# Self-attention of a decoder's second block: four score products of a batch in one group, and the sums of the softmax from TensorE

## The reference, cut to what matters

```
x = x @ Wq + bq (and Wk, Wv); q, k turned by rope
scores = jnp.einsum('bhqd,bhkd->bhqk', q, k) / np.sqrt(D_K)
probs = jax.nn.softmax(scores, axis=-1)
attn = jnp.einsum('bhqk,bhkd->bhqd', probs, v)
x = _layernorm(x + attn @ Wo + bo)
```

## Time and profile before

| | us |
|---|---|
| median of 3 runs | 2189.8 (2188.1 to 2191.36) |
| profiled execution | 2189.22 |
| its span | 2187.4 |
| granted clock of PE, mean | 0.947 |

### The profile page before, as it was taken

One profiled execution on the slowest core, in us unless ns is written; L12 is line 12 of the kernel. 1 busy time (PEld: TensorE's weight loads), 2 busy tenths in 40 slices (PEclk: granted clock), 3 DMA queues, 4 the chain that ended last, 5 costly groups with the idle time before them and its releaser, 6 DMA issues.

```text
span 2187.4 us, 46524 instructions
## 1 busy us (share of the span) xinstructions
PE 1948.0 (89%) x16008; PEld 1493.8 (68%) x16008; DVE 1409.0 (64%) x3579; ACT 1272.1 (58%) x4630; POOL 449.0 (21%) x777
## 2 busy tenths in 40 slices
PE   3549999999999999999689999889997777699998
PEld 1227888888888888888456767656665444467775
DVE  4776777777777777777356566467776577354443
ACT  2215666666666667776334444379997788133333
POOL 2101111111111111111222122034443233011110
PEclk8769999999999999999889999989999899599999
DMA  7000000000000000000200000010000000000000
GB/s 220 16 0 2 1 2 1 2 2 2 2 2 2 2 1 2 2 2 2 68 1 1 1 1 1 13 23 2 2 2 3 24 16 2 1 1 10 10 1 19
DMA packets 29436, 25.57 MB, mean 12 GB/s; under 512 B 5260, under 2 KB 25748, under 8 KB 29208
## 3 DMA queue, kind: packets, MB, share of 16 engines
q1 hardware_dynamic: 29208, 22.62, 3.6%
HBM read 20.52 MB, written 2.10 MB: 10 GB/s over the span
## 4 chain that ended last, share of the span: by engine, by line
issue 64%; PE 13%; POOL 8%; ACT 7%; POOLq 6%; DVE 1%; DMA 1%; DVEq 0%; SPq 0%; ACTq 0%
ACT work L1484 5%; POOL work L946 2%; PE bank L1950 2%; PE bank L1937 2%; PE bank L1419 2%; PE bank L1939 2%; ACT work L1492 2%; POOLq L949 1%; POOL H L950 1%; POOL work L934 1%; POOL work L1039 1%; PE bank L1918 1%; PE bank L1428 1%; POOLq L1830 1%; POOLq L1828 1%
## 5 line engine op out<-in xcount | busy, mean ns | idle before, releaser
L814 ACT ACTIVATE work<-bank,work 128x128 f32<-128x128 f32 x1024 | 364.6, 405 | 223.8 <-DVE work L867 223.8
L694 PE MATMUL bank<-work,wbig 128*128 128x128 f32 x2048 | 261.8, 276 | 0.6 <-ACT work L855 0.5
L814 ACT ACTIVATION_READ_ACCUMULATOR work<-bank,work 128x1 f32 x1024 | 250.6, 245 | 0.0
L694 PEld LDWEIGHTS bank<-work,wbig 128*128 128x128 f32 x2048 | 245.5, 193 | 1.2 <-ACT work L855 0.8
L874 DVE TENSOR_TENSOR work<-work 128x512 f32<-128x512 f32 x256 | 177.3, 692 | 24.3 <-issue 6.4
L867 DVE TENSOR_REDUCE work<-bank 128x4 f32<-128x512 f32 x256 | 158.9, 682 | 33.7 <-PE bank L733 33.7
L1484 ACT ACTIVATE work<-bank,work 128x128 f32<-128x128 f32 x512 | 176.0, 346 | 4.3 <-DVE work L1520 4.3
L829 ACT ACTIVATE work<-bank 128x512 f32<-128x512 f32 x256 | 170.4, 666 | 13.2 <-PE bank L707 13.2
L707 PE MATMUL bank<-ident,work 128*128 128x128 f32 x1024 | 156.4, 276 | 3.0 <-DVE work L874 3.0
L1173 ACT ACTIVATE work<-bank,col_b 128x512 f32<-128x512 f32 x128 | 87.2, 687 | 104.0 <-PE bank L1101 104.0
L2112 DVE TENSOR_TENSOR work<-work,bank 128x320 f32<-128x320 f32 (+1 forms) x128 | 62.4, 488 | 131.5 <-ACT work L2025 130.9
(11 more groups left out here) (287 smaller groups left out, 4075.4 us busy)
## 6 DMA issues: line engine op xcount, KB each, us to landing
wbig<-in_moe_w SPq DMA_DIRECT2D x2, 1536.0 KB, 9.3
work<-in_mask_l SPq DMA_DIRECT2D x8, 256.0 KB, 2.8
out<-X SPq DMA_DIRECT2D x8, 256.0 KB, 2.3
H<-in_moe_w SPq DMA_DIRECT2D x3, 512.0 KB, 5.7
wff<-in_moe_w SPq DMA_DIRECT2D x1, 1024.0 KB
wbig<-in_sa_wq SPq DMA_DIRECT2D x1, 512.0 KB, 3.8
wbig<-in_sa_wk SPq DMA_DIRECT2D x1, 512.0 KB, 4.6
wbig<-in_sa_wv SPq DMA_DIRECT2D x1, 512.0 KB, 6.1
```

The costliest lines, as they stand in the source:

```text
L694: last = nc.tensor.matmul(o[:, j * T:(j + 1) * T], w[:, t * 128:(t + 1) * 128], src, start=True, stop=True)
L814: last = nc.scalar.activation(at_probs[:, g, h, :], bank[g][:, h * T:(h + 1) * T], ACT.Exp, bias=at_nmax[:, g, h:h + 1], accum_out=at_den[ ...
```

## The change

The four score products of a batch are one group at the head of round t; their semaphore counts batches. `accum_out` goes, and with it the reciprocal of 128 x 16, its transpose, its copy and `l1_expand`. In their place stands `l1_ones`, [128, 4, 32], where block s holds ones in columns 8s to 8s+7: 16 more products with it in `weigh` give the sum of each head's exps already spread over the head's 8 lanes, in columns 128 to 255 of bank 7. `heads` takes the reciprocal of these 128 x 128 sums and multiplies. Orders change on PE (turn(t, 0) behind weigh(t-1)), on ACT (the copy of the last group, then tokens, then exps of group 0; exps of group 3 ahead of the copy of group 1) and on DVE (all four maxima first; the copy of group 2 at the end of its own round). The counts of waits and the takes of SBUF follow. The diff, cut to its core:

```
                 for k in range(2):
-                    nc.tensor.transpose(bank[5][:, k * T:(k + 1) * T], l1_turn[:, k, :], ident[:])
-                nc.tensor.transpose(bank[5][0:HEADS, 2 * T:3 * T], headmask[:, :], ident[:]).then_inc(l1.tables_ready, 1)
+                    last = nc.tensor.transpose(bank[5][:, k * T:(k + 1) * T], l1_turn[:, k, :], ident[:])
+                last.then_inc(l1.tables_ready, 1)
...
                 need(pe, l1.xT_sb, min(t + 3, B))
-                if t + 3 < B:
-                    last = nc.tensor.transpose(bank[7][:, 0:T], X[:, t + 3, :], ident[:])
-                if 1 <= t <= B:
-                    pe.wait_ge(l1.recips, t)
-                    last = nc.tensor.transpose(bank[7][0:HEADS, T:2 * T], l1_recip[(t - 1) % 2], ident[:])
-                if t + 3 < B or t >= 1:
-                    last.then_inc(l1.turned, 1)
+                nc.tensor.transpose(bank[7][:, 0:T], X[:, t + 3, :], ident[:]).then_inc(l1.turned, 1)
...
-            def score(b, pair):
+            def score(b):
                 pe.wait_ge(l1.kblk, b + 1)
-                need(pe, l1.probs, QUAD * (b - 1) + 2 * pair + 2)
-                for i in (2 * pair, 2 * pair + 1):
+                need(pe, l1.probs, QUAD * b)
+                for i in range(QUAD):
                     p = 32 * i
...
                 pe.wait_ge(l1.xT_sb, min(b + 4, B - 1) + 1)
-                pe.wait_ge(l1.recipT_sb, b + 1)
                 pe.wait_ge(l1.v_sb, b + 1)
-                for s in range(QUAD):
-                    for j in range(QUAD):
-                        nc.tensor.matmul(bank[7][32 * j:32 * j + 32, 0:T], l1_v[b % 3][:, s, 32 * j:32 * j + 32],
-                                         l1_probsT[b % 2][:, j, s, :], start=(s == 0), stop=(s == QUAD - 1),
-                                         skip_group_check=True)
-                nc.tensor.matmul(bank[7][:, T:2 * T], l1_expand, l1_recipT, start=True, stop=True).then_inc(l1.pv, 1)
+                for k, weights in enumerate((None, l1_v[b % 3])):
+                    for s in range(QUAD):
+                        for j in range(QUAD):
+                            w = weights[:, s, 32 * j:32 * j + 32] if k else l1_ones[:, s, :]
+                            last = nc.tensor.matmul(bank[7][32 * j:32 * j + 32, (1 - k) * T:(2 - k) * T], w,
+                                                    l1_probsT[b % 2][:, j, s, :], start=(s == 0), stop=(s == QUAD - 1),
+                                                    skip_group_check=True)
+                last.then_inc(l1.pv, 1)
...
                 if now:
-                    score(t, 1)
+                    score(t)
                 if t >= 1:
                     turn(t - 1, 3)
-                tokens(t)
+                if t + 3 < B:
+                    tokens(t)
                 if 0 <= t + 2 < B:
                     project(t + 2)
-                if now:
-                    turn(t, 0)
                 if t >= 1:
...
                 if now:
+                    turn(t, 0)
                     turn(t, 1)
-                if 0 <= t + 1 < B:
-                    score(t + 1, 0)
                 output(t)
...
                     last = nc.scalar.activation(l1_probs[b % 2][:, g, h, :], bank[g][:, h * T:(h + 1) * T], ACT.Exp,
-                                                bias=l1_nmax[b % 2][:, g, h:h + 1],
-                                                accum_out=l1_den[b % 2][:, QUAD * g + h:QUAD * g + h + 1])
+                                                bias=l1_nmax[b % 2][:, g, h:h + 1])
                 last.then_inc(l1.probs, 1)
...
                 act.wait_ge(l1.turned, t + 4)
-                if t + 3 < B:
-                    nc.scalar.activation(l1_xT[(t + 3) % 3], bank[7][:, 0:T], ACT.Copy).then_inc(l1.xT_sb, 1)
-                if 1 <= t <= B:
-                    need(act, l1.pv, t - 1)
-                    nc.scalar.activation(l1_recipT, bank[7][0:HEADS, T:2 * T], ACT.Copy).then_inc(l1.recipT_sb, 1)
+                nc.scalar.activation(l1_xT[(t + 3) % 3], bank[7][:, 0:T], ACT.Copy).then_inc(l1.xT_sb, 1)
...
                 now = 0 <= t < B
-                if now:
-                    exps(t, 0)
                 if t >= 1:
                     turned(t - 1, 3)
-                tokens(t)
+                if t + 3 < B:
+                    tokens(t)
+                if now:
+                    exps(t, 0)
                 if now:
...
                     exps(t, 2)
+                    exps(t, 3)
                     turned(t, 1)
-                    exps(t, 3)
...
             def greatest(b, g):
-                dve.wait_ge(l1.scores, 2 * b + g // 2 + 1)
+                dve.wait_ge(l1.scores, b + 1)
                 nc.vector.tensor_reduce(l1_nmax[b % 2][:, g, :], bank[g][:, :].rearrange("p (h t) -> p h t", h=QUAD),
                                         AX.X, ALU.max, negate=True).then_inc(l1.maxes, 1)
-
-            def recip(b):
-                dve.wait_ge(l1.probs, QUAD * (b + 1))
-                need(dve, l1.turned, b + 3)
-                nc.vector.reciprocal(l1_recip[b % 2], l1_den[b % 2]).then_inc(l1.recips, 1)
...
                 need(dve, l1.out_ready, b)
-                nc.vector.tensor_copy(l1_headsT, bank[7][:, 0:T])
-                dve.drain()
-                nc.vector.tensor_tensor(l1_headsT, bank[7][:, T:2 * T], l1_headsT, ALU.mult).then_inc(l1.heads_sb, 1)
+                nc.vector.reciprocal(l1_recip, bank[7][:, T:2 * T])
+                dve.drain()
+                nc.vector.tensor_tensor(l1_headsT, bank[7][:, 0:T], l1_recip, ALU.mult).then_inc(l1.heads_sb, 1)
...
                                         DH1 ** -0.5 if k < 2 else 1.0, None, ALU.mult)
-            nc.vector.tensor_copy(l1_expand, bank[5][0:HEADS, 2 * T:3 * T]).then_inc(l1.tables_sb, 1)
+            for k in range(QUAD):
+                nc.vector.memset(l1_ones[:, k, :], 0.0)
+            dve.drain()
+            for k in range(QUAD):
+                last = nc.vector.memset(l1_ones[:, k, DH1 * k:DH1 * (k + 1)], 1.0)
+            last.then_inc(l1.tables_sb, 1)
             dve.drain()
...
                 now = 0 <= t < B
-                if t >= 1:
-                    recip(t - 1)
-                    turned(t - 1)
-                if now:
-                    greatest(t, 2)
-                    greatest(t, 3)
+                if now:
+                    for g in range(QUAD):
+                        greatest(t, g)
                 if 0 <= t + 2 < B:
...
                     heads(t - 1)
-                if 0 <= t + 1 < B:
-                    greatest(t + 1, 0)
-                    greatest(t + 1, 1)
-                if t >= 1:
                     residual(t - 1)
...
                     values(t + 1)
+                if now:
+                    turned(t)
...
                 pool.wait_ge(l1.turned_halves, b + 1)
-                need(pool, l1.scores, 2 * (b - 1))
+                need(pool, l1.scores, b - 1)
                 nc.gpsimd.tensor_tensor(l1_qk[b % 2], l1_half[b % 2][:, :, 0, :], l1_half[b % 2][:, :, 1, :], ALU.add)
```

More of the change, by code:

```diff
@@ L242, in build @@
             xT_sb = sem("l1_xT_sb")
-            recipT_sb = sem("l1_recipT_sb")
             qk = sem("l1_qk")
@@ L249, in build @@
             probs = sem("l1_probs")
-            recips = sem("l1_recips")
             probsT = sem("l1_probsT")
@@ L1346, in build @@
         l1_wturned = r.take(2, D)
-        l1_expand = r.take(D, parts=HEADS)
+        l1_ones = r.take(QUAD, 4 * DH1)
         l1_xT = [r.take(T) for _ in range(3)]
@@ L1355, in build @@
         l1_nmax = [r.take(QUAD, QUAD) for _ in range(2)]
-        l1_den = [r.take(HEADS) for _ in range(2)]
-        l1_recip = [r.take(HEADS) for _ in range(2)]
-        l1_recipT = r.take(T, parts=HEADS)
+        l1_recip = r.take(T)
         l1_headsT = r.take(D)
@@ L1496, in tokens @@
                 act.wait_ge(l1.turned, t + 4)
-                if t + 3 < B:
-                    nc.scalar.activation(l1_xT[(t + 3) % 3], bank[7][:, 0:T], ACT.Copy).then_inc(l1.xT_sb, 1)
-                if 1 <= t <= B:
-                    need(act, l1.pv, t - 1)
-                    nc.scalar.activation(l1_recipT, bank[7][0:HEADS, T:2 * T], ACT.Copy).then_inc(l1.recipT_sb, 1)
+                nc.scalar.activation(l1_xT[(t + 3) % 3], bank[7][:, 0:T], ACT.Copy).then_inc(l1.xT_sb, 1)
             for t in range(-3, B + 1):
                 now = 0 <= t < B
+                if t >= 1:
+                    turned(t - 1, 3)
+                if t + 3 < B:
+                    tokens(t)
                 if now:
                     exps(t, 0)
-                if t >= 1:
-                    turned(t - 1, 3)
-                tokens(t)
                 if now:
```

## The result

| | us |
|---|---|
| median of 8 runs, changed | 2194.95 (2192.98 to 2198.09) |
| median of 8 runs, before | 2189.74 (2188.1 to 2191.36) |
| ratio | 1.0026, 95% interval 1.0016 to 1.0036 |
| profiled execution, changed | 2193.04, span 2191.3, mean clock 0.95 |

The account below looks back on a forecast made before the run. A ring of work between PE and ACT was taken to bound the kernel; a longer ring through weigh, less an earlier start, plus a later end gave +3.7 to +4.8 us: 2194.5 predicted, range 2179 to 2205.

Parts of the forecast that it names:

- The ring: Score group, ACT copies, weigh, turn 0, its copy, eight exps, back to PE: 8.04 us a batch against 7.854.
- The distance of two exps: On ACT, an exp without its accumulator read repeats after 0.25 to 0.26 us.
- A: Rival on ACT: an exp without its read repeats at 0.30; ring 8.35, +12.5 us, 2202; chance 0.18.
- B: Rival on ACT: an exp repeats like a Copy, 0.16; ring 7.41, -15 us, 2174; chance 0.12.
- the reciprocal: DVE's 128x128 reciprocal, 0.95 us, costs nothing in the ring; done twice, 0.6 of 0.95 would come through.
- C: Rival: PE sets the pace, batch takes PE's 6.7 us; -38 us, 2151; chance 0.03.
- D: Rival on DVE: the reciprocal comes through, over 1.5 us, or DVE's round reaches next maxima; +10, 2199; chance 0.07.
- ACT's idle time: ACT idles once a batch, about 1 us before turn 0's copy; idling before another instruction would show the forecast wrong.
- The work of both engines: Work per batch: ACT falls from 7.3 to 5.6 us, PE from 7.4 to 6.7.
- The second group: Start of the stage: the second score group starts near 1438.5, 3.3 us earlier; this term 2 us either way.
- The end: From the last score group to the stage's end: 17.9 us instead of 16.1, 1.8 more.
- The sum: Whole stage: -3.3 + 27 x 0.19 + 3 x 0.03 + 1.8 = +3.7 us; +4.8 with exps of 0.255.

Follow-up runs that it names:

- ones alone: Kernel before with no accumulator reads, sums by 16 products with ones and the 128x128 reciprocal; score pairs and old orders kept: 2182.4 us, ratio 0.9969.
- group alone: Kernel before with the four score products in one group and the changed orders; accumulator reads and spreading product kept, no ones: 2219.1 us, ratio 1.0138.
- exps 2 early: Changed kernel with one line moved on ACT, exps of group 2 before the copy of turn 0: 2172.9 us, ratio 0.9932.
- turn 2 early: Changed kernel with exps of group 2 before ACT's copy of turn 0, and turn 2 ahead of PE's output product, DVE reordered to match: 2170.4 us, ratio 0.9915.

## Why the prediction was right

**The ring, the main step, was right and 0.13 short.** Predicted against measured: group 1.06, 1.07; to ACT 0.69, 0.69; copy 0.49, 0.50; x and the wait for weigh 0.52, 0.52; weigh 1.86, 1.89; to ACT 0.70, 0.69; copy 0.48, 0.49; eight exps to the end of the last 2.09, 2.17; to PE 0.15, 0.15. Sum 8.04 against 8.17, just above the 8.0 to 8.1 that was named. Over half of what is missing is the last exp: I gave it 0.34 as in the kernel before, and it lasts 0.42. (The missing read isn't the reason: with the reads put back the last of eight lasts 0.41 to 0.42 too.) The distance of two exps, on which rivals A and B hung, is 0.25: (1568.71 - 1566.71) / 8. Their mean duration is 0.397, near A's 0.39, but they overlap by 0.15 on average, not 0.09. The Trainium skill (ScalarE: Activation LUTs, "What ACT_TABLE_LOAD costs") gives 93 ns of overlap, and from its figures comes the estimate of 294 ns; here the measurement decides, 250 ns, and only the duration agrees.

**The ring's existence is shown from three sides**: exps taken out of it (-0.87 us a batch), weigh shortened (-0.65), reads put into it (+0.72 where 0.66 was expected), the first as far as the next ring (7.30) lets it, the others in full where the clock is full. A piece outside it, the reciprocal, came through with 0.11 of 1.03; the prediction had 0.6 of 0.95, and was wrong there: PE's wait for the product is the 0.4 it had, but DVE had more room than it counted. C (PE's amount) is out for the changed kernel, where PE is busy 34.5 of 40, but is what bounds the ones alone. D didn't come: the reciprocal takes 0.957 us, as worked out.

**ACT's idle time was misread.** The prediction had ACT idle once a batch, about 1 us before the copy of turn 0, and named idle time before another instruction as a sign of being wrong. ACT idles 0.76 there and 1.42 before the copy of turn 3. The sign was wrong, not the ring: between the last exp and that copy the prediction's own terms have 0.15 + 1.06 + 0.69 us, of which ACT fills 0.48 with the copy of turn 1, and that leaves 1.42. The work of both engines was put too low as well (ACT 5.6 a batch, busy 6.04; PE 6.7, busy 7.05); these figures stand in rivals B and C, and in no term of the sum.

**Start and end.** The second group starts at 1438.30 (forecast 1438.5); counted from the stage's first copy on DVE (1418.10 before, 1417.78 after) that is 3.1 us earlier than the pair at 1441.75. The end I took as 1.8 longer; it is 0.4, from 1682.85 to 1699.35, 16.5 against 16.1. I had weigh at 2.8 on a half-risen clock, and it took 1.95 at full clock.

**The sum.** -3.1 + 30 x (8.152 - 7.854) + 0.4 = +6.2 for the stage, where 3.7 to 4.8 were predicted: against the 3.7 the ring was put too low by 3.7 us (by 2.7 with exps of 0.255), the start too early by 0.2 and the end too high by 1.4. The profiled span grew by 3.9 only. 0.3 lies ahead of the stage, and 2.0 behind it: from its end to the end of the span 493.9 us before, 492.0 after, in stages whose code is the same. The first 80 us or so of the last stage went at a granted clock of 0.69 before and 0.73 after (starts of the windows shifted by 5.9 us):

```profile
1870.00:1950.00 80.00, 62.99 (x231) 44.23 (x232) 33.30 (x81) 18.31 (x38) 7.95 (x11) 0.69 0.00 1
```

```profile
1875.90:1955.90 80.00, 62.92 (x249) 43.92 (x249) 34.42 (x84) 20.13 (x41) 7.95 (x11) 0.73 0.00 1
```

and eight runs of the changed kernel spread over 5.1 us. So the close hit of the median, 0.45 us, is partly luck; what is shown is a stage 6 us longer, and what the clock adds or takes elsewhere stays open.

**Where the expected gain went.** The longest ring is another one in each kernel:

| kernel | us a batch | what sets the pace |
|---|---|---|
| before | 7.85 | ring through ACT with twelve exps and their reads |
| ones alone | 7.69 | PE's work |
| group alone | 8.77 | ring through ACT with all sixteen exps and their reads |
| changed | 8.17 | ring through weigh, turn 0 and eight exps |
| changed, exps 2 early | 7.30 | ring through ACT with sixteen exps, and DVE's round |

The ones save 7 us with the old orders. The group with its orders costs 30 while the reads are there, and 12 on top of the ones (7 + 5). PE's 1.06 us a batch saved by four quarters are real and off the path. Together +5: without the reads ACT's own ring falls to 7.30, and what remains longer is the way through weigh, which the ones made 0.87 longer, and turn 0 behind it. With one line of ACT's order changed both halves are used: 2173, and 2170 with turn 2 early, 0.7% and 0.85% below before. Whether turn 0 put back ahead of weigh on PE would do the same was not tried.

## What to carry to other kernels

When two engines are each 94% busy and each waits once per round, write down the ring that joins them before counting what a change removes: what an edit takes off an engine pays only if it lies in that ring or in the next longest one. A larger group saves its engine's time and makes one consumer's last piece gate the producer, and pieces that had been done ahead now stand in the ring; check what stands in front of that last piece in the consumer's hand-written order, above all a copy that waits for the producer's newest work. When such a ring appears, reorder first: here one line was worth four times the whole effect of the change.

## What the runs showed of the hardware

- An activation of 128x128 with a bias column repeats after 0.25 us, with its accumulator read after 0.343. In the changed kernel each of a row of eight lasts 0.008 longer than the one before it, from 0.36 to 0.42, while the distance stays 0.25. With the reads put back it is the same, while in the kernel before and with the group alone each lasts 0.34 to 0.36; the cause is open.
- Sixteen products of 32 output lanes in four column quarters, 32 instructions, take 1.01 us, and 64 take 1.89: 0.027 for each more. It is the same whether products with ones are added or products with values left out.
- PE's clock isn't told by its busy share alone: with the reads put back PE was busy 33.1 of 40 us at a clock of 0.87, with the group alone 30.7 of 40 at 1.00 (the row below). The wait before the score group is 0.8 us in both. Which of PE's waits makes the difference stays open.

```profile
1480.00:1520.00 40.00, 30.69 (x342) 22.20 (x340) 27.03 (x74) 34.32 (x175) 16.86 (x26) 1.00 0.01 2
```
